# Two halves of an attention's scores issued together on TensorE in a four-stage transformer pipeline

## The reference

```python
# first block
x1 = x  + attention(LN1(x) @ w_qkv, mask_1x1xSxS)          @ w_ao + b_ao   # stage A, self attention
x2 = x1 + attention(q = LN2(x1) @ w_q, kv = ctx @ w_kv, mask_Bx1xSxS) @ w_co + b_co  # stage B, first cross attention
x3 = x2 + gelu(LN3(x2) @ w1 + b1) @ w2 + b2                # stage M, the MLP, 1024 inner features
# second block
y  = x3 + tanh(gate) * (attention(q = x3 @ Wq.T, kv = LN(ctx) @ Wk.T, Wv.T, key mask) @ Wo.T)  # stage C, second cross

def attention(q, k, v, mask):
    scores = einsum('bhqd,bhkd->bhqk', q, k) / sqrt(16)
    scores = scores * mask - 10000.0 * (1.0 - mask)        # C: -inf where the key mask is off
    return einsum('bhqk,bhkd->bhqd', softmax(scores), v)
```

## Time and profile before

| | us |
|---|---|
| median of 3 runs | 963.01 (961.67 to 965.79) |
| the profiled execution | 968.34 |
| its span, first to last instruction | 966.5 |
| busy: PE / PEld | 884.2 / 827.5 |
| busy: DVE / ACT / POOL | 696.9 / 576.2 / 560.1 |
| granted TensorE clock, mean | 0.956 |

### The profile page before, as it was taken

How to read it: one execution, slowest core, us unless ns; L and a number is a source line. 1 busy time by engine, 2 the same in 40 slices (tenths; PEclk the granted TensorE clock), 3 DMA queues, 4 the chain that set the end, 5 groups by cost and what they waited for, 6 DMA issues and landing times.

```text
span 966.5 us, 24365 instructions
## 1 busy us (share of the span) xinstructions
PE 884.2 (91%) x9808; PEld 827.5 (86%) x9808; DVE 696.9 (72%) x1463; ACT 576.2 (60%) x1073; POOL 560.1 (58%) x565
## 2 busy tenths in 40 slices
PE   5678789999999999999999999999999999998885
PEld 5577788999999898989999998989999998987774
DVE  4366767779697877878697877878787877775533
ACT  4235555758484766658584856657584847665342
POOL 1327383939476574929475675929385765836221
PEclk9657999999999999999999999999999999998996
DMA  6021000010101010010101010010101010000000
GB/s 213 1 67 40 23 19 12 2 52 1 41 13 41 13 30 24 2 52 2 41 12 42 12 41 13 1 53 1 52 1 42 13 41 2 24 19 1 24 12 12
DMA packets 33005, 26.74 MB, mean 28 GB/s; under 512 B 12672, under 2 KB 32000, under 8 KB 32896
## 3 DMA queue, kind: packets, MB, share of 16 engines
q1 hardware_dynamic: 32896, 25.20, 8.9%
HBM read 20.99 MB, written 4.19 MB: 26 GB/s over the span
## 4 chain that ended last, share of the span: by engine, by line
PE 51%; DVE 31%; issue 6%; POOL 6%; ACT 4%; DMA 1%; SPq 0%; DVEq 0%; ACTq 0%; POOLq 0%
PE pj L418 15%; PE pj L436 10%; PE s_bank L499 8%; PE s_bank L485 6%; DVE prob_AC L893 5%; PE s_bank L474 4%; PE pj L449 4%; DVE vz_AC L885 3%; DVE h_hi L1097 3%; DVE rmax_B L898 3%; DVE stats L933 2%; DVE x L917 2%; DVE oT_AC_lo L863 2%; POOL h_lo L1139 2%; DVE vz_B L885 2%
## 5 line engine op out<-in xcount | busy, mean ns | idle before, releaser
L1112 POOL TENSOR_TENSOR rstd<-var_eps,half 128x2 f32<-128x2 f32 x64 | 47.5, 743 | 233.3 <-DVE var_eps L944 233.3
L1132 POOL TENSOR_TENSOR prob_AC<-prob_AC,rmax_C 128x512 f32<-128x512 f32 x64 | 66.2, 1046 | 111.6 <-DVE rmax_C L898 109.2
L707 ACT ACTIVATE k<-pj,kbias,consts 128x256 f32<-128x256 f32 x192 | 93.0, 572 | 51.1 <-PE pj L418 51.1
L474 PE MATMUL s_bank<-k,q 64*128 64x128 f32 x1536 | 107.4, 284 | 7.6 <-ACT q L694 3.9
L474 PEld LDWEIGHTS s_bank<-k,q 64*128 64x128 f32 x1536 | 92.4, 188 | 19.7 <-ACT q L691 6.4
L1139 POOL TENSOR_TENSOR h_lo<-g,h_hi 128x512 fp32r<-128x512 f32 x64 | 83.7, 1328 | 9.8 <-DVE h_hi L1097 9.8
L1126 POOL TENSOR_TENSOR prob_B<-prob_B,maskB_off 128x512 f32<-128x512 f32 x64 | 81.3, 1304 | 11.3 <-DVE prob_B L893 11.3
L1126 POOL TENSOR_TENSOR prob_AC<-prob_AC,maskA_off 128x512 f32<-128x512 f32 x64 | 80.7, 1285 | 5.2 <-DVE prob_AC L893 5.2
L485 PE MATMUL s_bank<-consts,prob_AC 128*128 128x128 f32 x512 | 71.7, 285 | 12.3 <-POOL prob_AC L1132 12.3
L449 PE MATMUL pj<-w_hi_M,h_hi 128*128 128x256 f32 x256 | 77.8, 304 | 5.0 <-issue 3.3
L715 ACT ACTIVATE prob_AC<-s_bank 128x512 f32<-128x512 f32 x128 | 68.1, 596 | 17.6 <-PE s_bank L485 17.4
(11 more groups left out here) (195 smaller groups left out, 3001.1 us busy)
## 6 DMA issues: line engine op xcount, KB each, us to landing
x_in<-in_x SPq DMA_DIRECT2D x16, 256.0 KB, 2.7
ctx_b<-in_ctx_features SPq DMA_DIRECT2D x16, 256.0 KB, 3.0
ctx_c<-in_ctx SPq DMA_DIRECT2D x16, 256.0 KB, 3.3
out<-y SPq DMA_DIRECT2D x16, 256.0 KB, 2.2
g<-in_w_M SPq DMA_DIRECT2D x2, 1024.0 KB, 6.8
maskB<-in_mask_Bx1xSxS_ff SPq DMA_DIRECT2D x32, 64.0 KB, 2.7
prob_AC<-in_w_A_qkv SPq DMA_DIRECT2D x1, 768.0 KB, 4.5
prob_B<-in_w_B_kv SPq DMA_DIRECT2D x1, 512.0 KB, 6.2
```

Of the source, the lines that this page charges most:

```text
L474: mm = nc.tensor.matmul(bank[:, c, :, b2, :], q2[rows_, c, t * TILE + b2].rearrange("p e q -> p (e q)"), k2[rows_, c, t * TILE + b2], star ...
L707: last = nc.scalar.activation(k2[:, m, :, s, :], k_all[:, m], ACT.Identity, bias=kbias[:, "ABC".index(a), s, m:m + 1], scale=parity[:, 2 + ...
L1132: nc.gpsimd.tensor_tensor(p3, p3, rmax[a][:, r, :].unsqueeze(2).broadcast_to([P, BL * TILE, S]), ALU.subtract).then_inc(shifted[a], 1)
```

## The change

The order of instructions on TensorE is changed at two places of `body`; nothing else is. No instruction is added or taken away. At the first place the first half of the scores of C stands behind the transposes M.zT, next to the second half. At the second place the first half of the scores of B stands behind M.H2, next to the second half.

```diff
-                if active("C", i):
-                    scores("C", 0, i)
                 if active("M", i):
                     pe.wait_ge(ln_done["M"], unit("M", i) + 1)
                     turn("M.zT", z["M"], i)
                 if active("C", i):
+                    scores("C", 0, i)
                     scores("C", 1, i)
                 if active("B", i):
                     pe.wait_ge(ln_done["B"], unit("B", i) + 1)
...
                     feature_major("M.H1", i)
                     feature_major("M.H0", i)
+                    feature_major("M.H2", i)
                 if active("B", i):
                     scores("B", 0, i)
-                if active("M", i):
-                    feature_major("M.H2", i)
-                if active("B", i):
                     scores("B", 1, i)
                 if active("C", i):
                     turn_probs("C", 0, i)
```

## The result

The changed kernel takes 973.67 us in the median of 5 runs (971.97 to 976.2), the kernel before beside it 964.73: a ratio of 1.0100 (95% interval 1.0074 to 1.0126). It is slower, as forecast, by some 9 us where 6.2 was said. 973.67 lies just above the forecast's own range of 965 to 973, which was counted from 963.0; the rise of 8.9 us lies inside the 2.3 to 10.3 that the range was made of, and 973.67 inside the wider 957 to 976.

A forecast was written before the change was run, and what follows sets the result against it. The chain was taken to alternate between TensorE and VectorE, with GpSimd pacing the second place; twelve middle bodies 5.2, body 3 +1.35, body 16 -0.3 made 6.2 us, 963.01 becoming 969.2. Own range 965 to 973, wider 957 to 976.

The forecast's parts named there:

- First place, 0 us: Scores of C: joining saves TensorE about 0.3 us, worth nothing in middle bodies because B.Q waits for VectorE's gapless run.
- Second place, GpSimd's offsets 0.45 us later: Scores of B: mask B0 1.43 us later against 0.97 us reserve; offsets 0.45 us later, middle body about 0.43 longer.
- Whether DVE is 0.6 or 0.9 us late doesn't matter, GpSimd's end does.: Second place: `mean_neg` ends with GpSimd's fourth offset, 499.92 instead of 499.48, however late VectorE reaches it.
- The last cast of M: Worst case, second place: with its GELU earlier it holds up GpSimd's shift B3 some 0.3 us; body +0.7.
- Body 3, +1.35 us: Stage C absent, nothing covers GpSimd: the whole 1.43 us reaches its offsets; +1.35 us, bounds 0.6 to 1.45.
- Body 16, -0.3: ScalarE decides; its third GELU waited 0.74 us for M.H2, now earlier; -0.3 us, bounds -0.7 to +0.4.
- Body 17, 0: VectorE waited for B.zT: the first place gives up to 0.5 us, cancelling the second's 0.45.
- The sum: Whole kernel: 5.2 + 1.35 - 0.3 = 6.2 us on 968.34, giving 974.5, ratio 1.0064; median 963.01 becomes 969.2.
- absorption (1): Rival, chance 0.16: VectorE's 1.0 us of "issue" at `mean_neg` is reserve and soaks up the delay; 963 us.
- the return of TensorE's savings (2): Rival, chance 0.08: TensorE's 0.7 us saved per body comes through over 15 bodies, 10.5 us; 952.5 us.
- a GpSimd instruction earlier (3): Rival, chance 0.08: VectorE reaches `mean_neg` before the fourth offset starts, about 0.5 us less per body; 957 us.
- one more instruction late (4): Rival, chance 0.06: VectorE misses the fourth offset's end and waits for a 1.05 us shift; 982 us.

The follow-up runs named there:

- experiment 1: Only the first place changed (scores of C behind the transposes M.zT), against the kernel before: middle body 53.79 us, ratio 0.9991.
- 9: Kernel before with GpSimd's residual of B ahead of its shifts of C, plus the change's first place: body 53.27 us, 954.81 us, ratio 0.9916.
- Experiment 4: Changed kernel with `maskC_off` ahead of mask B0 on VectorE: middle body 54.17 us instead of 54.37, ratio to the kernel before 1.0042.
- Experiment 3: Kernel before with one additional GpSimd instruction ahead of the offsets of B: middle body longer by 0.33 us, ratio up by 0.6%.
- 7: Kernel before with both halves of B's scores ahead of M.H2: middle body 54.41 us, ratio 1.0038.
- 10: Kernel before with GpSimd's residual of B ahead of its shifts of C and both halves of B's scores ahead of M.H2: middle body 53.68 us.
- 5: Kernel before with GpSimd's residual of B ahead of its shifts of C: middle body 53.27 us, 956.41 us, ratio 0.9911.
- 11: Residual of B early, B's score halves ahead of M.H2, C.OT's parts moved earlier, VectorE's third cast behind both normalisations; against kernel before: body 54.72 us, ratio 1.0165.
- experiment 2: Only the second place changed (M.H2 ahead of both halves of B's scores), against the kernel before: middle body 54.35 us, ratio 1.0068.
- 6: Changed kernel with GpSimd's residual of B ahead of its shifts of C: middle body 54.34 us.
- 8: Changed kernel with VectorE's third cast behind the second normalisation of C: middle body 54.17 us, 0.20 less than without the edit.

## Why the prediction was right, and where its numbers were off

*What bounds the kernel* held. The chain goes to and fro between TensorE and VectorE, and the 0.37 and 0.38 us spared on TensorE in a middle body shortened nothing.

*First place, 0 us.* Right: shown alone by experiment 1 (53.79 us, 0.9991) and again by 9. The saving was put at about 0.3 us and is 0.37, the wait before B.Q at about 0.7 us and is 0.76.

*Second place, TensorE 0.40 us ahead.* Right: 0.38, all of it waiting before turn_out.

*Second place, GpSimd's offsets 0.45 us later.* The mechanism was right, the reserve mis-sized. I took 0.97 us with 0.08 for the signal; from the end of mask B0 (497.97 + 0.68) to the first offset (498.81) it takes 0.16, so the reserve was 0.89 and mask B0's 1.42 us of delay left 0.53. That is the body's 0.53, against the 0.43 of the forecast, within its bounds of 0.2 to 0.7: 1.2 us over twelve bodies.

*"Whether DVE is 0.6 or 0.9 us late doesn't matter, GpSimd's end does."* This sentence was wrong. Experiment 4 took VectorE's lateness away and left GpSimd's, and the body fell by 0.20 us. Experiment 3 gave GpSimd more delay (0.70) and VectorE none, and cost 0.33. That both of my errors, the signal and this one, left the sum near the measured one is partly luck: with GpSimd late by 0.51 and VectorE on time, the body would have been 54.17. What VectorE is late by decides which of GpSimd's instructions its `mean_neg`, `var_eps` and casts meet, and they cost differently.

*The last cast of M*, the upper bound's fear, cost nothing in the end. It now runs at once, in 0.42 us, and GpSimd gives way for 0.18 (the product of 128x2 takes 0.38 instead of 0.20), so shift B3 is 0.75 us later than before. The three low parts behind it, 3.76 us instead of 3.95, give it back. In the mean of the twelve bodies the offset of A0 is 0.53 us later, as the offset of B0 is (0.52).

*Body 3, +1.35 us.* The offsets there start 12.35 us after vz_B, before 10.92, so the whole 1.43 us did reach them. What it did to the body is not settled, since TensorE's clock is not yet full in it and differs between executions. Without late scores the body took 52.1 us at a mean granted clock of 0.97 (before and experiments 7, 9 and 10), but 53.2 to 56.4 at 0.90 to 0.92 (1, 3, 5 and 11); with them 53.6 to 54.1 at 0.93 to 0.94 (after, 2 and 4) and 54.7 to 54.8 at 0.91 (6 and 8). No kernel with late scores ran it at 0.97.

*Body 16, -0.3*: -0.18 (53.03 to 52.85). *Body 17, 0*: -0.43, from vz_B to the first matmul of C.Q 48.93 to 48.50 us at the same clock. The first place gave the 0.5 us (0.60 in experiment 1), but the second didn't take its 0.45 back (48.81 in experiment 2).

*The sum.* The profiled execution grew by 6.2 us, from 968.34 to 974.53, where 974.5 was forecast. That this fits to 0.1 us is luck: the two executions had unlike mean clocks, 0.956 and 0.961, and the 1.55 us that the changed one was shorter up to body 3 have nothing to do with the forecast. The medians differ by 8.9 (ratio 1.0100 against 1.0064 forecast, which lies below the interval's 1.0074), of which the middle bodies make 6.4. Most of the other 2.5 goes with the granted clock. Of the 68 runs of the kernel before that stand beside the experiments, the 29 with a mean clock of 0.965 took 963.4 us in the median, the 12 with 0.962 took 965.5, the 10 with 0.958 took 968.9. The changed kernel's five had 0.958 to 0.962. Against runs of the same clock they are 6.7 us longer (two at 0.962, 972.1) and 7.3 (one at 0.958, 976.2). With 6.4 for the middle bodies and -0.6 for bodies 16 and 17, some 0.9 to 1.5 us are left for body 3: an estimate, near the 1.35 of the forecast. Whether the change itself brings the lower clock is not shown.

Of the rivals, absorption (1) is excluded by the 0.53 us a body; the return of TensorE's savings (2) by the two longer waits and experiment 1; a GpSimd instruction earlier (3) did not happen in the changed kernel. Experiments 3 and 4 produced it, `mean_neg` ending with the third offset (501.35 + 0.75 and 498.29 + 0.52), and without its gain: `var_eps` or the next cast then waited for the fourth offset; one more instruction late (4) would have been 1 us a body.

## What to carry to other kernels

When work is moved behind other work to make one engine more efficient, look first at what its result releases on the slower engines, and at the slack of that release: here 0.4 us were saved on TensorE, and a signal moved 1.43 us against a reserve of 0.89. A body that ends on VectorE can be set by GpSimd without its name in the chain: unexplained "issue" of an odd length on a tiny VectorE instruction, which ends when a GpSimd instruction ends, is the sign to look for. And here an idle stretch on the engine that set the pace was worth more than a cheaper order on the other: moving one 1.27 us instruction into GpSimd's idle time gave 0.9%.

## What the runs showed of the hardware

VectorE's tensor_scalar of 128x256 from uint8 takes 0.28 us beside an idle GpSimd and 1.06 us when it starts 0.37 us after a GpSimd tensor_tensor of 1.28; tensor_scalar on 128x2 takes 0.17 us, and up to 1.26 in the kernel before. A cast of 128x512 takes 0.41 us at best and 1.5 at most, with a median of 1.10 before and 0.42 after. Tensor_tensor from PSUM with a mask (0.68) and tensor_reduce (0.67 to 0.69) kept their times in every kernel, beside busy and idle GpSimd alike. It goes the other way too: in the changed kernel a GpSimd product of 128x2 beside the fourth cast took 0.38 us instead of 0.20:

```profile
509.48 0.42 DVE L1094 CAST h_hi<-g 128x512 fp32r<-128x512 f32 x1
```
```profile
509.58 0.38 POOL L1111 TENSOR_TENSOR mrstd<-mean_neg,rstd 128x2 f32<-128x2 f32 x1
```

This is what the Trainium skill (SBUF — State Buffer, "Who interferes with whom") describes for the port pair that the two engines share. Its effect on the schedule here: in the rows shown each such wait ends with a GpSimd instruction of 1.0 to 1.3 us. That fits the finding that a delay of 0.70 us cost 0.33 a body and one of 0.51 together with a late VectorE 0.53; that it is the whole reason is argued, not shown.

On TensorE, 32 score matmuls of half the rows in one run take 1.98 us against 2 x 1.09 in two, and the 12 matmuls of M.H2 between two groups of scores 1.62 us against 1.43. At each place two changes between half-height and full-height matmuls fell away, and 0.37 and 0.38 us with them. The Trainium skill (TensorEngine Tiling (Array Packing), "Key Properties") has a drain at a change of tiling mode; the trace agrees, with about 0.19 us for each change.
